# First attention rebuilt: host-ordered tokens, a front per block between the heads, and exponentials stationary in the value product

## The reference

```
x = x + L0_conv_ref(ln(x), qkv_w, qkv_b, proj_w, proj_b, rel_pos_h, rel_pos_w)   # windows 14x14
t = t + L0_ffn_ref(ln(t), ...)       # 8 experts, 2 per token
x = x + L1_conv_ref(ln(x), ...)      # dilated 3x3 attention
t = t + L1_ffn_ref(ln(t), ...)       # 8 experts, 2 per token
```

```
xp = pad(x to 28 x 28); win = xp in windows of 14 x 14          # 4 windows an image
q, k, v = win @ qkv_w.T + qkv_b
attn = (q * scale) @ k.T
attn += rel_h[:, :, :, :, None] + rel_w[:, :, :, None, :]        # from q, rel_pos_h, rel_pos_w
out = softmax(attn) @ v
out = out @ proj_w.T + proj_b;  cropped back to 16 x 16
```

## Time and profile before

| | |
|---|---|
| median of 3 runs | 1086.57 us |
| the profiled execution | 1082.64 us |
| its span, first to last instruction | 1080.8 us |
| mean granted clock of PE | 0.847 |
| busy share PE, PEld, DVE, ACT, POOL | 72%, 62%, 52%, 30%, 41% |
| first attention, start to the first transposes of the stage behind (L295 at 370.08) | 370 us |

### The profile page before, as it was taken

One profiled execution on the slowest core, in us unless ns is written; L12 is line 12 of the kernel. 1 busy time (PEld: TensorE's weight loads), 2 busy tenths in 40 slices (PEclk: granted clock), 3 DMA queues, 4 the chain that ended last, 5 costly groups with the idle time before them and its releaser, 6 DMA issues.

```text
span 1080.8 us, 18138 instructions
## 1 busy us (share of the span) xinstructions
PE 782.3 (72%) x5320; PEld 664.9 (62%) x5321; DVE 564.3 (52%) x1124; ACT 326.1 (30%) x718; POOL 441.6 (41%) x737
## 2 busy tenths in 40 slices
PE   4980699898989726999999256044448269999991
PEld 2470598787889416999999134011126159999991
DVE  5233667576674564333332540999955653333324
ACT  1752354244433212333333032000003123333330
POOL 0203342321320124666665331367711246666651
PEclk9965599899899766999999676578978669999996
DMA  8144443333220381111111317930019301111115
GB/s 225 32 152 124 75 86 63 58 68 68 39 36 2 108 349 29 48 48 46 50 51 37 116 47 151 183 57 19 19 36 386 114 29 50 48 46 50 48 37 175
DMA packets 65265, 92.06 MB, mean 85 GB/s; under 512 B 23380, under 2 KB 47028, under 8 KB 64504
## 3 DMA queue, kind: packets, MB, share of 16 engines
q1 hardware_dynamic: 55176, 69.24, 24.8%
q0 software_dynamic: 10048, 22.31, 7.0%
HBM read 66.98 MB, written 25.81 MB: 86 GB/s over the span
## 4 chain that ended last, share of the span: by engine, by line
PE 53%; DVE 27%; DMA 7%; issue 6%; POOL 3%; ACT 2%; SPq 2%; DVEq 0%; POOLq 0%; ACTq 0%
PE ps L1054 12%; PE ps L1062 9%; PE ps L1066 6%; PE ps L639 5%; DVE rt L1335 4%; PE ps L1592 2%; PE ps L644 2%; DVE qq L483 2%; DVE x_sb L1001 2%; DVE xn L1328 2%; DVE arena L1328 2%; DMA qd<-arena 2%; PE ps L1045 2%; PE ps L1395 2%; PE ps L295 2%
## 5 line engine op out<-in xcount | busy, mean ns | idle before, releaser
L1108 ACT ACTIVATE arena<-ps,b1s 128x128 f32<-128x128 f32 x468 | 129.5, 375 | 213.3 <-PE ps L1066 133.7
L1054 PE MATMUL ps<-arena 128*128 x936 | 165.4, 327 | 1.5 <-DVE rt L969 1.5
L1054 PEld LDWEIGHTS ps<-arena 128*128 128x128 f32 x936 | 150.3, 190 | 2.4 <-issue 2.1
L433 POOL TENSOR_TENSOR kk<-arena,kk 16x1536 fp32r<-16x1536 f32 x16 | 64.7, 4041 | 142.6 <-ACT kk L744 142.5
L1062 PE MATMUL ps<-xnT 128*128 128x128 f32 x936 | 120.1, 279 | 2.3 <-DVE xnT L962 2.3
L1062 PEld LDWEIGHTS ps<-xnT 128*128 128x128 f32 x936 | 116.8, 195 | 3.7 <-DVE xnT L962 3.7
L1405 PE MATMUL ps<-xnT,cst 128*128 128x512 f32 (+3 forms) x88 | 45.1, 644 | 66.0 <-POOL xnT L1287 66.0
L1120 POOL TENSOR_TENSOR credit<-credit 1x1 f32<-1x1 f32 x306 | 56.9, 186 | 79.8 <-DVE rt L969 35.4
L1287 POOL TENSOR_TENSOR xnT<-arena,rt 128x1024 f32<-128x1024 f32 (+3 forms) x21 | 65.5, 3144 | 50.2 <-DVE rt L1362 38.0
L1128 POOL DMA_INDIRECT xnT<-xnd,gcur x78 | 78.6, 1008 | 15.7 <-issue 14.7
L639 PE MATMUL ps<-arena 98*102 98x196 f32 x384 | 80.4, 357 | 0.0
(11 more groups left out here) (197 smaller groups left out, 1413.8 us busy)
## 6 DMA issues: line engine op xcount, KB each, us to landing
arena<-in_w SPq DMA_DIRECT2D x16, 576.0 KB, 10.4
arena<-in_w1a SPq DMA_DIRECT2D x16, 384.0 KB, 10.6
arena<-yd SPq DMA_DIRECT2D x8, 768.0 KB, 7.2
arena<-kd SPq DMA_DIRECT2D x48, 96.0 KB, 5.8
arena<-qd SPq DMA_DIRECT2D x16, 264.0 KB
arena<-qd SPq DMA_DIRECT2D x16, 192.0 KB
arena<-in_w1b SPq DMA_DIRECT2D x16, 192.0 KB, 10.9
qkvd<-arena SPq DMA_DIRECT2D x32, 96.0 KB
```

What stands on the lines that cost most here:

```text
L433: nc.gpsimd.tensor_tensor(dst, fk[cc % 2][R_DUP:R_DUP + HD], dst.bitcast(F32), ALU.subtract)\
L1054: last = mm(ps[:, DOWN, 0:C], hidT[r][:, f, :], w2s[:, e, f, :], start=f == 0, stop=f == FT - 1)
L1108: last = nc.scalar.activation(hidT[r][:, f, :], hidden(r, f), ACT.Gelu, bias=b1s[l][:, bass.ds(e * FT + f, 1)])
```

## The change

The host hands x in window order and puts the output back from it, so that the kernel's token order in the first attention is that of the windows. In the kernel:

- The front is made per block. Its parts are `transposes` (x0, x1), `queries_and_keys` (t0, t1, t2), `relative` (r0, r1, r2) and `values` (v0, v1). Block 0's parts come at the start; those of block b+1 stand on PE between the heads 0 to 4, 7 and 8 of block b, each through the one bank `MISC`, which ACT or DVE has to empty before the next part may begin.
- `relative` has 64 matmuls a block of 32 moving elements each, with 112, 64 or 56 columns of weights; before there were 64 in all, of 128 moving columns.
- ACT rounds as it copies out of PSUM (L864, L865, L874), POOL takes the differences (L517, L526, L528) and issues 16 stores a block (L505). SP reads a chunk straight into `q0` and `k0`, in 7 transfers; `round_q`, `round_k`, `q_low` and `k_low` are gone.
- `values_product` has the exponentials as the stationary operand, eight times 98x98 and three times 120x120, and the 17 columns of one head's values and ones as the moving one. The result has tokens in the partitions. DVE divides by the sums there (98x24 and 120x6 reciprocals a group); `transposed_outputs` (L763) turns the group's result for the projection, whose bias comes in as a row.
- There are three buffers of exponentials instead of two. `scores_for_max` stays six heads ahead.
- Behind the first attention the copies of the normed tokens into transposed order before the dilated attention, and those of its result, are split in six pieces each, from window order to image order or back.

Two things of the loop on PE below: `ahead` is true while there is a next block, `behind` while there is one before; `s` is the head within the block.

```diff
-        qd = dram("qd", [NH, QROWS, T])
-        kd = dram("kd", [NH, HD, T])
-        kpd = dram("kpd", [NH, HD, PADS])
+        qd = dram("qd", [BLKS, QDROWS, NH, BT])
+        kd = dram("kd", [BLKS, 2 * HD, NH, BT])
...
+                for r, lo, hi in ((0, 0, 32), (R_DUP, 0, HD), (R_REL2, 32, QLO), (R_LO, QLO, QDROWS)):
+                    sp.dma_start(q0[r:r + hi - lo, cc].bitcast(F32), qd[b, lo:hi, hs]).then_inc(s_(f"chunk_in{cc}"), 16)
+                for r, lo in ((R_HI, 0), (R_DUP, HD), (R_LO, 0)):
+                    sp.dma_start(k0[r:r + HD, cc].bitcast(F32), kd[b, lo:lo + HD, hs]).then_inc(s_(f"chunk_in{cc}"), 16)
...
+            def heads_split(kind, b):
+                m = int(kind[1])
+                pool.wait_ge(s_("act_emptied"), EMPTIED[kind, b])
+                if m < 2:
+                    rows = P if m == 0 else P // 2
+                    for o, s in zip(natural_pieces(qf[0:rows, m]), window_pieces(src_w[0:rows, m])):
+                        last = nc.gpsimd.tensor_copy(o, s)
+                    last.then_inc(s_("qf_ready"), 1)
+                nc.gpsimd.tensor_tensor(src_lo[:, m], src_w[:, m], src_hi[:, m].bitcast(F32), ALU.subtract)\
+                    .then_inc(s_("split"), 1)
+                pool.wait_ge(s_("split"), split_at(kind, b))
+                store(kind, b)
...
+            def normalise(b, g):
+                n = b * 2 + g
+                v.wait_ge(s_("pv_done"), (n + 1) * HG)
+                o = ps[:, PV, 0:5 * HG * VW].rearrange("p (k h n) -> p k h n", k=5, h=HG)
+                nc.vector.reciprocal(rc[0:WAH, 0:4], o[0:WAH, 0:4, :, HD])
+                nc.vector.reciprocal(rc[0:NB, 4], o[0:NB, 4, :, HD]).then_inc(s_("rc_ready"), 1)
+                v.wait_ge(s_("rc_ready"), n + 1)
+                nc.vector.tensor_tensor(o_tok[0:WAH, 0:4, hs], o[0:WAH, 0:4, :, 0:HD],
+                                        rc[0:WAH, 0:4].unsqueeze(3).broadcast_to([WAH, 4, HG, HD]), ALU.mult)
+                nc.vector.tensor_tensor(o_tok[0:NB, 4, hs], o[0:NB, 4, :, 0:HD],
+                                        rc[0:NB, 4].unsqueeze(2).broadcast_to([NB, HG, HD]), ALU.mult)\
...
+            def relative(b, m):
+                bank = bank_of(f"r{m}", b)
+                pe.wait_ge(s_("qf_ready"), b * 2 + (2 if m == 2 else 1))
+                for at in range(SIDE):
+                    for w in range(2):
+                        if m < 2 and w != m:
+                            continue
+                        rows, r0 = (P, 0) if m < 2 else (P // 2, w * (P // 2))
+                        cols = H0 * WS if m < 2 else P // 2 if w == 0 else P // 2 - HD // 2
+                        q = qf[0:rows, m // 2].rearrange("p (i y x) -> p i y x", i=2, y=SIDE)
+                        o = ps[r0:r0 + cols, bank, :].rearrange("p (i y x) -> p i y x", i=2, y=SIDE)
+                        last = mm(o[:, :, at, :] if w == 0 else o[:, :, :, at], relt[w][0:rows, at % WS, 0:cols],
+                                  q[:, :, at, :] if w == 0 else q[:, :, :, at], start=True, stop=True)
+                last.then_inc(s_("misc_full"), 1)
...
-            def values_product(blk, cc, j):
-                h = cc * HC + j
-                n = blk * NH + h
-                if cc % 2 == 0 and j == 0:
-                    pe.wait_ge(s_("os_ready"), blk * 2 + cc // 2)
-                pe.wait_ge(s_("exp_done"), n + 1)
-                g, hh = h // HG, h % HG
-                at = slice(hh * VW, (hh + 1) * VW)
-                x, y = pa[h % 2], pb[h % 2]
-                first = hh == 0
+            def values_product(H):
+                b, h = H // NH, H % NH
+                hh = h % HG
+                if hh == 0:
+                    pe.wait_ge(s_("o_ready"), H // HG)
+                    pe.wait_ge(s_("dve_emptied"), EMPTIED["v1", b])
+                pe.wait_ge(s_("exp_done"), H + 1)
+                x, y, v_ = pa[H % 3], pb[H % 3], v0[b % 2]
+                o = ps[:, PV, 0:5 * HG * VW].rearrange("p (k h n) -> p k h n", k=5, h=HG)
                 for i in range(2):
                     for c in range(2):
-                        mm(ps[0:VW, PV, i * WA:(i + 1) * WA], v0[0:WAH, g, 2 * i + c, at],
-                           x[0:WAH, i, c * WA:(c + 1) * WA], start=first, stop=False, skip_group_check=True)
-                        first = False
+                        for kc in range(2):
+                            mm(o[0:WAH, 2 * i + c, hh], x[0:WAH, i, kc * WA + c * WAH:kc * WA + (c + 1) * WAH],
+                               v_[0:WAH, 2 * i + kc, h], start=(hh, i, c, kc) == (0, 0, 0, 0), stop=False,
+                               skip_group_check=True)
                 for c in range(3):
-                    vs = v0[0:NB, g, 4, at] if c == 0 else vpad[0:NB, g, at]
-                    last = mm(ps[0:VW, PV, 2 * WA:BT], vs, y[0:NB, c], start=False, stop=hh == HG - 1 and c == 2,
+                    vs = v_[0:NB, 4, h] if c == 0 else vpad[0:NB, h]
+                    last = mm(o[0:NB, 4, hh], y[0:NB, c], vs, start=False, stop=hh == HG - 1 and c == 2,
                               skip_group_check=True)
...
+                    scores(H)
+                    if ahead and s == 0:
+                        transposes(b + 1, 0)
+                    if ahead and s == 1:
+                        queries_and_keys(b + 1, 0)
+                    if ahead and s == 2:
+                        relative(b + 1, 0)
+                    if ahead and s == 3:
+                        queries_and_keys(b + 1, 1)
+                    if ahead and s == 4:
+                        relative(b + 1, 2)
+                    if ahead and s == 7:
+                        values(b + 1, 0)
+                    if ahead and s == 8:
+                        values(b + 1, 1)
+                    if H + AHEAD < HEADS:
+                        scores_for_max(H + AHEAD)
+                    if s % HC == 0 and H // HC + 1 < BLKS * CPB:
+                        transposed_maxima(H // HC + 1)
+                    if s == 1 and behind:
+                        transposed_outputs(b - 1, 1)
+                    if s == 7:
+                        transposed_outputs(b, 0)
+                    if H:
+                        values_product(H - 1)
+                    if ahead and s == 0:
+                        transposes(b + 1, 1)
+                    if ahead and s == 1:
+                        queries_and_keys(b + 1, 2)
+                    if ahead and s == 2:
+                        relative(b + 1, 1)
+                    if behind and s == 3:
+                        projection(b - 1, 0)
+                    if behind and s == 4:
+                        projection(b - 1, 1)
+            values_product(HEADS - 1)
+            transposed_outputs(BLKS - 1, 1)
+            projection(BLKS - 1, 0)
+            projection(BLKS - 1, 1)
...
-            def round_q(blk, n):
-                cc = n % CPB
-                act.wait_ge(s_(f"fq_in{n % 2}"), (blk * 2 + n // 2 + 1) * 64)
-                nc.scalar.activation(q0[0:R_ROUND, cc], fq[cc % 2][0:R_ROUND], ACT.Copy).then_inc(s_("q_rnd"), 1)
-            def round_k(blk, n):
-                cc = n % CPB
-                act.wait_ge(s_(f"fk_in{n % 2}"), (blk * 2 + n // 2 + 1) * 48)
-                nc.scalar.activation(k0[0:R_ROUND, cc], fk[cc % 2][0:R_ROUND], ACT.Copy).then_inc(s_("k_rnd"), 1)
...
+            def round_heads(b, m):
+                act.wait_ge(s_("misc_full"), FULL[f"t{m}", b])
+                bank = bank_of(f"t{m}", b)
+                nc.scalar.activation(src_w[:, m], ps[:, bank, :], ACT.Identity, bias=bqk0[:, m:m + 1])
+                nc.scalar.activation(src_hi[:, m], ps[:, bank, :], ACT.Identity, bias=bqk0[:, m:m + 1])\
...
-                nc.scalar.activation(yT[b % 2], ps[0:KC, u:u + 2, :], ACT.Copy).then_inc(s_("yT_ready"), 1)
+                for k in range(2):
+                    for o, s in zip(window_pieces(yT[b % 2][:, k]), natural_pieces(ps[0:KC, u + k, :])):
+                        last = nc.scalar.activation(o, s, ACT.Copy)
+                last.then_inc(s_("yT_ready"), 1)
```

More of the change, by code:

```diff
@@ L192, in build @@
[L192 to L201, removed]
+        src_hi = ar(0, [3, BT]).bitcast(F32R)
+        src_lo = ar(3 * BT, [3, BT]).bitcast(F32R)
@@ L337, in permute @@
[L337 to L344, removed]
-        ST_A, ST_B, SM_A, SM_B, PV, MISC = 0, 2, 3, 5, 6, 7
[L355 to L366, removed]
-        def attn0_sync(sp):
[L369 to L416, removed]
@@ new lines, in build, with bank_of, ln0_statistics @@
+        FULL, EMPTIED, BEFORE = {}, {}, {}
+        emptied, before = {"act_emptied": 0, "dve_emptied": 0}, None
+        for n, use in enumerate(misc_uses()):
+            by = "act_emptied" if use[0][0] in "xtro" else "dve_emptied"
+            emptied[by] += 1
+            FULL[use], EMPTIED[use], BEFORE[use] = n + 1, emptied[by], before
+            before = by, emptied[by]
+        def bank_of(kind, b):
```

(57 more changed lines are left out.)

844 lines of the change are left out of this document (432 added, 412 removed).

## The result

The changed kernel takes 1228.5 us, median of four runs (1227.3 to 1233.4), beside 1088.0 for the kernel before on the same chips (1085.9 to 1090.6): a ratio of 1.130 with a 95% interval of 1.126 to 1.134. It is slower, by some 140 us; 1220 was forecast.

What follows compares the result with a forecast made beforehand. PE was taken to bound the heads. Start 70, heads 422 and tail 9 gave 501 against 370, +131, with +3 behind +134: 1216.6 profiled, 1220 stated. Its own range was 1150 to 1270, the overall range 1015 to 1260.

Steps and rivals of the forecast that it cites:

- The value product: Per head, 22 passes of 17 moved columns: 3.9 us lower, 2.0 upper, counted at +0.2 us a head, not a gain.
- the second rival: Value product: passes of 17 columns are cheap, 1.3 us a head, 34 us off the first rival, 1001 us; chance 0.08.
- The clock: PE over the heads: at the lower level for most heads, 6.4 us a step, clock 0.55 to 0.65.
- The heads: First attention, heads with fronts between: 466 us all lower, 246 all upper, taken as 422.
- the front: A block's transposes, q and k, relative products and values: 40 us lower, 20 upper, three times between the heads.
- the share given back: Heads: dense parts lift the level now and then, so a fifth of the lower-upper difference comes off, 466 - 44.
- The start: Before the first scores, block 0 alone goes first: 70 us instead of 127, bounds 60 and 85.
- The bank and the chunks: PE's waits in the heads: 10 us for bank MISC (0 to 24); chunk reads covered, if not 0 to 15 a block.
- What goes: q_low's waits and the roundings go: 3.4 us at each of seven places, some 25 us gained.
- The tail: From the last value product to L295: 9 us instead of 16.7, bounds 7 and 12.
- Behind it: Copies in six pieces around the dilated attention: +3 us over four blocks, bounds 0 and 8.
- The first rival: Clock stays at the upper level in the heads: 62 + 246 + 8 = 316, 1035 us stated; chance 0.22.

Runs made afterwards that it cites:

- The one edit in the kernel before: The kernel before with only the value product changed: exponentials stationary, 17 columns moved, taken from the bias row instead of the values; 1214.0 us, ratio 1.118.
- the version with both dense: Changed kernel, value product moving the head's 17 columns up to six times over (93 on average), relative products 96 columns instead of 32; 1057.4 us, ratio 0.975.
- the dense product alone: Changed kernel with the same 22 passes and weights, each value product pass moving the head's 17 columns up to six times over, 93 on average; 1076.4 us, ratio 0.992.
- the version with values stationary: Changed kernel with the value product turned back: a group's 102 columns of values stationary, 196 or 120 columns of exponentials moving, 14 passes a head; 1063.5 us, ratio 0.980.

## Why the prediction was right

**The value product** was priced at 3.9 us lower and 2.0 upper; it takes 3.77 and 1.96. The cheap passes of the second rival (1.3 us) did not come. The 25 ns a pass that the Trainium skill gives for few moving columns ("TensorE: Matmul & The Clock Gate", "Back-to-back issue gap") would have made it 0.55 us. That section says itself that its figure for a single matmul has no weight load in it and comes out too low for few columns; behind a full load of weights the trace shows 0.083 us a pass.

**The clock** was the step on which the sign hung, and it was read from L1614, which fell with PE busy by the records. It held: 0.52 over the heads (0.55 to 0.65 was said), with PE busy for 98.8% of them. The one edit in the kernel before (0.91 to 0.50) and the four widths of the moving operand (17, 31, 60 and 93 columns: 0.52, 0.54, 0.71 and 0.88 over the heads) show that it is the columns moved. The Trainium skill ("TensorE: Matmul & The Clock Gate", Part 1) ties the clock to how busy PE is; by its letter the heads would have stayed at the upper level, and the trace disagrees: 98.8% busy at a clock of 0.52.

**The heads** came out at 426.5 us for 422, but by two errors that cancel. Taken from the timeline, the list at the lower level is 48 x 6.23 = 299 less 7 for the maxima made ahead, three fronts 104, maxima turned 13, outputs 6, six half projections 16, waits 7: 438, not 466. The mis-sized term is the front, 35 us for 40, and in it the relative products. r2's 64 passes of 64 rows were put at 0.11 by their columns; the windows of L677 alone have r0, then r2 (us, PE busy, PEld busy, clock):

```profile
95.20:101.00 5.80, 5.79 (x32) 5.80 (x32) 0.50 0.34 74
124.50:128.00 3.50, 3.49 (x64) 3.48 (x64) 0.50 0.82 223
```

5.80/32 = 0.18 us for 112 columns and 3.50/64 = 0.055 for 64 and 56. The rest is the step (8 us) and the waits. Against that the share given back was too large: a fifth of the difference, 44 us, where 438 less the measured 426.5 leaves 11.5 for upper stretches of 17 us in all. So the list was 28 us too long and the share given back 32 too large; that the sum is within 5 us is luck, the level and the step's cost are not.

**The start** is 74.7 for 70. The last relative product ends at 42.84, where 14 and 26 made 40; storing and reading back takes 15.3 from there to the first maxima, where 10 were taken; and the six maxima take 16.6 for 20 (PE's timeline of r2; chain of waits: start us, us, what; PE's timeline of the maxima):

```profile
39.22 3.62 PE L677 MATMUL ps<-xnT,arena 64*64 64x32 f32 x64 [2.27 <-POOL xnT L515]
```

```profile
49.18 8.71 DMA kk<-kd
```

```profile
58.14 0.95 PE L702 MATMUL ps<-kk,qq 114*98 114x196 f32 x4 [6.01 <-DMA kk<-kd]
...
61.04 0.98 PE L702 MATMUL ps<-kk,qq 114*98 114x196 f32 x4 [1.50 <-DVE rt L565]
```

The maxima began at 58 us, not 50; each still takes 2.9 with DVE's 1.5 in it, as in the earlier trace rows.

**The bank and the chunks.** All of PE's waits on other engines between 74 and 515 us (us in total, times, longest us):

```profile
PE ps L774 <- DVE x_sb L603: 2.9, 1, 2.9
PE ps L677 <- ACT arena L865: 1.8, 3, 0.8
PE ps L650 <- DVE nm L571: 1.5, 1, 1.5
PE ps L702 <- DVE rt L565: 1.5, 1, 1.5
PE ps L763 <- DVE arena L596: 1.3, 1, 1.3
PE ps L763 <- ACT arena L865: 1.0, 2, 0.8
PE ps L774 <- ACT xnT L879: 0.8, 1, 0.8
PE ps L752 <- ACT arena L865: 0.8, 3, 0.3
```

For the bank MISC that is under 5 us where 10 were taken, and none for a chunk: POOL and its stores are covered, as said. At the upper level the cover is thinner; the version with both dense waits 0.84 us for a chunk once at 120 us, the dense product alone 2.11, and the version with values stationary 3.6.

**What goes.** The 25 us put down to q_low are too many for PE: over the heads of before it was idle for 18.3 us in all (228 less 209.66). The forecast does not rest on it, since its list has no such wait.

**The tail** is 11.9 for 9. The reciprocals did shrink; what stays is a chain of layer norm and projections:

```profile
501.62 0.31 DVE rt L591
...
507.17 2.71 DVE xn L282 x8
509.88 0.47 DVE x_sb L603
510.36 0.14 issue
510.49 2.90 PE ps L774 x8
```

**Behind it** the split copies are 1.32 us for 1.02 in the earlier trace rows:

```profile
761.22 1.32 ACT L321 ACTIVATE xnT<-ps 96x392 f32<-96x392 f32 x6 [4.36 <-PE ps L298]
```

0.3 us each, less than the 0.5 to 1.0 assumed, and 2 us in all for 3.

**The first rival** was priced right in its large term. With all dense the heads take 327 - 75.4 = 252 us where 246 were listed; but it comes to 1057, not 1035. Of the 22 us, 13 are the start: 62 were taken, and it is 75 at either level of the heads, since the maxima before them stay at the lower level. The heads are 6 of them, the tail 3.

## What to carry to other kernels

When an operand is swapped so that few columns move past many weights, count the weight loads first: here they set the pace, and the moved columns that were saved gained nothing. Then look at the granted clock: here PE was busy for 99% of a stretch by the records and ran at half speed, while its largest part moved 17 columns a pass. If so, try passes that move more, even columns that are overwritten later; behind 98 columns of weights they cost nothing here, and they gave back some 150 us. With that done, look for PE's longest waits: the one fall that was left followed a wait of 2.26 us for a transfer.

## What the runs showed beside that

Passes of 64 rows with 64 or 56 columns of weights, written to the lower and the upper half of the partitions in turn, come every 0.055 us at the lower level and every 0.032 at the upper (64 in 2.05 us with values stationary), under the 0.047 that 56 columns would need at the pace of L739's 98 in 0.083. With 96 moved columns instead of 32 they come every 0.049 at the upper level (64 in 3.14 us), so there, unlike behind a full load of weights, the moved columns are not free.
